# Parts of the output projection as jobs of the attention stage, edges fetched first, and two narrow one-hots in five made by GpSimd

## The chip, the cores and the metric

The kernel runs on one core of a Trainium2 chip. The metric is the device time of one execution in microseconds (us). Engines are named as in the profile: PE (TensorE), DVE (VectorE), ACT (ScalarE), POOL (GpSimd), SP (SyncE, which here only issues DMAs).

## The reference

Two layers run over 1250 nodes with 512 features; each layer adds a graph part and an attention part to x.

```python
edge_index = jnp.stack([src, dst])          # 41250 edges, sorted by dst
deg = jnp.maximum(segment_sum(ones, dst, 1250), 1.0)
x = x + L0_gnn(_layernorm(x), wc, wn, bias, edge_index)   # x@wc + mean over edges of (x@wn) + bias
x = x + L0_ffn(_layernorm(x))               # causal attention, 8 heads, then 8 gated experts
x = x + L1_gnn(_layernorm(x), src, dst, deg, W_self, W_neigh, bias, gamma, beta)
x = x + L1_ffn(_layernorm(x))               # below
# L1_ffn: x += conv3(x); q, k, v = x @ qkv_w.T + qkv_b, 8 heads of 64
logits = (q * c**-0.5) @ k.T;  _, idx = top_k(logits, 16)
attn = softmax(logits at idx);  out = attn @ v at idx
return out @ wo_w.T + wo_b
```

## The kernel before

The nodes are ten tiles of 128 rows (NT), the features four blocks of 128 (KD). Stages follow each other as blocks; in a block each engine has its own instruction stream in the order of the code, and semaphores order the engines.

**The edge stage** is `graph_in`. It builds the dense count of edges between all node pairs. SP first issues eight DMAs for src and dst (the tile `raw`), then at once those of `wc`, the biases, `wn` and the q, k, v weights; ACT issues the DMAs of X. DVE splits each edge's source into a remainder and a quotient by 128 and takes the target relative to a window (`part`, `key`); the smallest and largest give a flag that says whether every edge lies in its window. PE transposes three key blocks of three tiles each, DVE copies the result to `ends`. DVE and PE then read the flag as a register and branch: here the `Else` branch runs. It goes over 323 tiles of 128 edges (ET). For each, DVE makes two one-hots by comparing a ruler with a per-partition number: a narrow one, `hot_b`, 128 columns, and a wide one, `hot_m`, 240 columns (L263 and L264). PE multiplies them into a bank of counts (L380). Eight buffers of each are in turn (HOTS = 8), so the one-hots of tile t wait until PE has used tile t - 8 (`s_used`). Finished banks of 51 targets are copied by ACT (L466). Beside this ACT normalises the rows of X, POOL makes the rest `lo` of their split into two f16 parts (L211), and PE multiplies them with `wc`.

**The top attention stage** is `top_layer`. It goes over n = 0 to 79, that is 8 heads by 10 tiles of rows. DVE finds the 16 largest of 1250 logits of each row with two maxima and two replacements (L1683 to L1691), ACT takes exponentials, POOL subtracts, PE transposes and weighs. ACT copies the finished heads' outputs from the bank `ps_o` (`drain`), POOL scales them (`normalise`) into QO. In odd n, PE does a job in the same bank: the projections of the next heads' q, k and v, and from n = 61 the transposes of the output weight (`work_at`, `job`, ACT's `keep_job`). In the last iterations and behind them PE multiplies QO with the weight, four matmuls for each of the ten tiles (`project`), DVE adds each to X, and SP stores it.

## Time and profile before

| | us |
|---|---|
| median of 3 runs | 1689.25 (1688.99 to 1690.77) |
| the profiled execution's own time | 1686.05 |
| its span in the profile | 1684.2 |
| mean granted clock of PE | 0.966 of full speed |

The span is from the first to the last instruction of the profiled execution; its own time has some microseconds around it. Times in the rows are counted from the start of the span. A row of the order of time gives start, length, engine, line, operation, tiles and shape, and in brackets how long the engine was idle before it and what ended that.

### The profile page before, as it was taken

To read this page: it belongs to the slowest core of one execution; us is meant where nothing else is said; L and a number is where in the kernel's file an instruction comes from. 1 tells how busy PE (TensorE), PEld (TensorE's weight loads), DVE (VectorE), ACT (ScalarE), POOL (GpSimd) and SP (SyncE) were. 2 spreads that over 40 slices of the span, in tenths; PEclk is the share of its full clock that TensorE was granted. 3 is DMA by queue.
4 is the path that set the end of the run, shared out by engine and by line. 5 is a ranking of instruction groups with operands and counts; after the bars stand their busy time and mean duration, and the time that the engine had idled before them with its cause. 6 is when DMAs were issued, how large, how long until landed. Compare 5 with 4: busy or idle time off the path is not lost. (4 is left out here: it accounts for less than half of the span.)

```text
span 1684.2 us, 22128 instructions
## 1 busy us (share of the span) xinstructions
PE 1486.9 (88%) x8227; PEld 928.2 (55%) x8227; DVE 1027.9 (61%) x2001; ACT 723.4 (43%) x1396; POOL 541.6 (32%) x399
## 2 busy tenths in 40 slices
PE   4888988997878789999999899777999999998778
PEld 2444534445666654454546545455776776776554
DVE  6999233327777721113223324748999999999981
ACT  4442013225565621111111220235778778778771
POOL 0113200015565410000000060007876667577550
PEclk9999989999999999999999999889999999999999
DMA  6001000025212050000000200011101100120001
GB/s 232 1 1 79 0 1 1 0 63 158 57 39 56 9 204 24 0 0 0 1 0 0 76 1 0 1 31 33 32 1 32 32 13 20 33 53 5 1 1 61
DMA packets 28570, 57.01 MB, mean 34 GB/s; under 512 B 7904, under 2 KB 12644, under 8 KB 28208
## 3 DMA queue, kind: packets, MB, share of 16 engines
q1 hardware_dynamic: 27152, 53.03, 11.5%
q10 hardware_dynamic: 1312, 2.56, 0.4%
q8 instruction: 68, 1.11, 0.3%
q14 instruction: 38, 0.31, 0.1%
HBM read 28.77 MB, written 5.84 MB: 21 GB/s over the span
## 5 line engine op out<-in xcount | busy, mean ns | idle before, releaser
L1285 POOL TENSOR_TENSOR tl_ex<-tl_ex,tl_left 128x1250 f32<-128x1250 f32 x80 | 209.8, 2622 | 37.0 <-ACT tl_left L1587 32.9
L1126 DVE SCALAR_TENSOR_TENSOR X<-ex_ps_x,g,X 128x512 f32<-128x512 f32 x80 | 59.9, 750 | 192.6 <-PE ex_ps_x L1019 192.6
L1406 PE MATMUL tl_banks<-identf,tl_ex 128*128 128x128 f32 x800 | 139.4, 290 | 42.1 <-ACT tl_pt L1608 25.6
L1608 ACT COPY tl_pt<-tl_banks 128x512 f32<-128x512 f32 (+1 forms) x200 | 108.1, 541 | 83.8 <-PE tl_banks L1406 80.8
L992 PE MATMUL ex_ps_h<-yt,w 128*128 128x512 f32 (+1 forms) x384 | 143.8, 529 | 0.0
L1406 PEld LDWEIGHTS tl_banks<-identf,tl_ex 128*128 128x128 f32 x800 | 90.0, 144 | 97.3 <-ACT tl_pt L1608 44.3
L1019 PE MATMUL ex_ps_x<-w,hid 128*128 128x512 f32 (+1 forms) x320 | 143.1, 599 | 0.0
L1072 ACT ACTIVATE hid<-ex_ps_h,b 128x512 f32<-128x512 f32 (+1 forms) x48 | 29.1, 608 | 242.2 <-PE ex_ps_h L992 242.2
L1899 POOL TENSOR_TENSOR lo<-xn,hi 128x512 f16<-128x512 f32 x5 | 5.9, 1186 | 379.5 <-ACT hi L1989 379.5
L1587 ACT ACTIVATE tl_left<-tl_left,tl_negm 128x1250 f32<-128x1250 f32 x80 | 107.5, 1343 | 29.2 <-DVE tl_left L1691 28.8
L1683 DVE MAX8 tl_m<-tl_banks 128x8 f32<-128x1250 f32 x80 | 116.3, 1454 | 5.7 <-PE tl_banks L1383 5.6
L1689 DVE MAX8 tl_m<-tl_left 128x8 f32<-128x1250 f32 x80 | 117.1, 1464 | 2.8
L1687 DVE MATCH_REPLACE8 tl_left<-tl_m,tl_banks 128x1250 f32<-128x1250 f32 x80 | 116.0, 1450 | 0.0
L1691 DVE MATCH_REPLACE8 tl_left<-tl_m,tl_left 128x1250 f32<-128x1250 f32 x80 | 115.6, 1445 | 0.0
L992 PEld LDWEIGHTS ex_ps_h<-yt,w 128*128 128x128 f32 x384 | 74.5, 195 | 65.8 <-issue 65.6
L1581 ACT ACTIVATE tl_ex<-tl_banks,tl_negm 128x1250 f32<-128x1250 f32 x80 | 104.7, 1309 | 2.4 <-DVE tl_left L1687 1.3
L1421 PE MATMUL tl_banks<-tl_pt,tl_V 128*64 128x128 f32 x1600 | 104.8, 278 | 0.0
L1019 PEld LDWEIGHTS ex_ps_x<-w,hid 128*128 128x128 f32 (+1 forms) x320 | 60.3, 189 | 74.0 <-issue 73.9
L1421 PEld LDWEIGHTS tl_banks<-tl_pt,tl_V 128*64 128x64 f32 x1600 | 85.7, 137 | 14.2 <-issue 14.2
L264 DVE TENSOR_SCALAR hot_m<-ruler,ends 128x240 f16<-128x240 f16 x323 | 92.6, 287 | 0.2 <-issue 0.2
L1340 PE MATMUL tl_banks<-tl_ct,tl_wt 128*128 128x512 f32 (+1 forms) x192 | 82.0, 554 | 9.3 <-DVE tl_ct L1658 6.2
L624 PE MATMUL ca_banks<-wqkv,ht 128*128 128x512 f32 x160 | 76.6, 625 | 12.7 <-DVE ht L804 12.7
(272 smaller groups left out, 2935.5 us busy)
## 6 DMA issues: line engine op xcount, KB each, us to landing
...
```

The lines of the kernel that those rows point to most:

```text
L992: mm = pe.matmul(h_bank(u)[:, 0:w], w1[e][:, k, j * P:(j + 1) * P], yt[:, G % 2, k, 0:w], start=(k == 0), stop=(k == KD - 1))
L1019: mm = pe.matmul(x_bank(v)[0:rows(t), :], hid[:, (EX * G + e) % HIDS, j, r * P:r * P + rows(t)], w2[:, 2 * e + j, :], start=(j == 0), stop ...
L1285: pool.tensor_tensor(ex[:, n % EXS, 0:N], ex[:, n % EXS, 0:N], left[:, n % LEFT, :], ALU.subtract).then_inc(s_probs, 1)
L1406: mm = pe.transpose(ps_t[:, b * P:(b + 1) * P], ex[:, n % EXS, a + b * P:a + (b + 1) * P], m.identf[:, :])
L1421: mm = pe.matmul(ps_o[u * DH:(u + 1) * DH, 0:P], V[:, h // 2 % 2, k, h % 2 * DH:(h % 2 + 1) * DH], pt[:, (2 * j + u) % PTS, k * P:(k + 1) ...
L1581: act.activation(ex[:, n % EXS, 0:N], logits(n)[:, 0:N], ACT.Exp, bias=negm[:, n:n + 1]).then_inc(s_exp, 1)
L1587: act.activation(lf, lf, ACT.Exp, bias=negm[:, n:n + 1]).then_inc(s_rest, 1)
L1608: act.copy(pt[:, n % PTS, a:a + w], ps_t[:, 0:w]).then_inc(s_kept, 1)
L1683: dve.max(m8[:, n % TOPS, 0:8], logits(n)[:, 0:N]).then_inc(s_max, 1)
L1687: dve.match_replace(lf, m8[:, n % TOPS, 0:8], logits(n)[:, 0:N], TAKEN).then_inc(s_read, 1)
L1689: dve.max(m8[:, n % TOPS, 8:16], lf).then_inc(s_max2, 1)
L1691: dve.match_replace(lf, m8[:, n % TOPS, 8:16], lf, TAKEN).then_inc(s_topped, 1)
```

## The change

Top attention: four jobs that transpose the output weight move from n = 61, 63, 65, 67 to n = 57 to 63. The weight is fetched at the start of the stage, into four vectors that earlier stages have done with. New jobs "out" at n = 65, 67, ..., 79 do, for tiles 0 to 7, the three of four matmuls whose heads are done by then; ACT copies the result to `partial`, POOL adds it to X one or two iterations later. `project` has one matmul left for these tiles and four for tiles 8 and 9.

Edge stage: SP's and ACT's other DMAs wait until the edges have landed. The keys come ahead of the flag; the third key block is made in the other branch alone. POOL makes `hot_b` of tile t, from t = 8 on, where t is 1 or 3 modulo 5 and no multiple of 8: 110 of the 323 tiles. POOL waits for `s_used` of tile t - 8, and PE waits for POOL's and DVE's semaphores. POOL's other work of the stage, `shift` and the ten `lo`, stands between these one-hots.

```diff
@@ -125,6 +126,7 @@
             if t in at and (kind, at[t][0] if kind == "own" else at[t]) not in side:
                 side[kind, at[t][0] if kind == "own" else at[t]] = len(side)
 
+    by_pool = [t for t in range(HOTS, ET) if t % HOTS and t % 5 in (1, 3)]
     used, counted = [], 1
     for t in range(ET):
         counted += closes[spans(t)[-1][0]] != t
@@ -173,6 +175,7 @@
                     "(a p) -> a p", a=1)).then_inc(s_edges, 16)
+            sp.wait_ge(s_edges, 16 * 2 * (EG + 1))
             sp.dma_start(wc[:, :, :], rows_of(io["L0_gnn_wc"])).then_inc(s_wc, 16)
@@ -204,11 +207,30 @@
                                base=0, pattern=[[-1, P]], channel_multiplier=1).then_inc(s_made, 1)
             pool.affine_select(out=m.padded[:, NT - 1:NT], in_=m.padded[:, NT - 1:NT], compare_op=ALU.is_ge,
                                fill=1.0, base=TAIL - 1, pattern=[[0, 1]], channel_multiplier=-1).then_inc(s_made, 1)
-            pool.wait_ge(s_inv, 1)
-            pool.tensor_tensor(m.shift[:, :], st[:, 1, :], m.scale[:, :], ALU.mult).then_inc(s_scaled, 1)
-            for t in range(NT):
+
+            def half_hot(t):
+                pool.wait_ge(s_used, used[t - HOTS])
+                if by_pool.index(t):
+                    pool.wait_ge(s_half_hot, by_pool.index(t))
+                pool.tensor_scalar(hot_b[:, t % HOTS, :], m.ruler[:, 0:P], ends[:, 0, t:t + 1], None, ALU.is_equal
+                                   ).then_inc(s_half_hot, 1)
+
+            def shifts():
+                pool.wait_ge(s_inv, 1)
+                pool.tensor_tensor(m.shift[:, :], st[:, 1, :], m.scale[:, :], ALU.mult).then_inc(s_scaled, 1)
+
+            def low(t):
                 pool.wait_ge(s_high, t + 1)
                 pool.tensor_tensor(lo[:, t, :], xn[:, t % XR, :], hi[:, t, :], ALU.subtract).then_inc(s_low, 1)
+
+            pool.wait_ge(s_cols, 1)
+            for t in range(ET):
+                if t in by_pool:
+                    half_hot(t)
+                if t == INVERT_AT + HOTS:
+                    shifts()
+                if t - LOW_AFTER in rows_at:
+                    low(rows_at[t - LOW_AFTER])
 
         @block.vector
         def _(dve):
@@ -236,17 +258,15 @@
             dve.wait_ge(s_split, 3)
+            dve.tensor_copy(key[:, 0, :, :], part[:, 0, :, :]).then_inc(s_split, 1)
+            dve.scalar_tensor_tensor(out=key[:, 1, :, :], in0=key[:, 3, :, :], scalar=float(NT), in1=part[:, 1, :, :],
+                                     op0=ALU.mult, op1=ALU.add).then_inc(s_split, 1)
             drel = key[:, 3, :, :].rearrange("p g e -> p (g e)")
             dve.tensor_reduce(worst[:, 0:1], drel, AX_X, ALU.max).then_inc(s_flag, 1)
             dve.tensor_reduce(worst[:, 1:2], drel, AX_X, ALU.min, negate=True).then_inc(s_flag, 1)
             dve.wait_ge(s_flag, 2)
             dve.scalar_tensor_tensor(out=worst[:, 2:3], in0=worst[:, 0:1], scalar=float(1 - WIN), in1=worst[:, 1:2],
                                      op0=ALU.add, op1=ALU.max).then_inc(s_flag, 1)
-            dve.tensor_copy(key[:, 0, :, :], part[:, 0, :, :]).then_inc(s_split, 1)
-            dve.scalar_tensor_tensor(out=key[:, 1, :, :], in0=key[:, 3, :, :], scalar=float(NT), in1=part[:, 1, :, :],
-                                     op0=ALU.mult, op1=ALU.add).then_inc(s_split, 1)
-            dve.scalar_tensor_tensor(out=key[:, 2, :, :], in0=raw[:, 1, :, :], scalar=float(NT), in1=part[:, 1, :, :],
-                                     op0=ALU.mult, op1=ALU.add).then_inc(s_split, 1)
             dve.wait_ge(s_lined, 1)
             dve.tensor_reduce(flag[:, 0:1], ps_w[:, 0:P], AX_X, ALU.max).then_inc(s_flag, 1)
             dve.wait_ge(s_flag, 4)
@@ -254,13 +274,14 @@
-            dve.tensor_copy(ends[:, :, :].rearrange("p n e -> p (n e)"), ps_f[:, 0:3 * EG * P]).then_inc(s_cols, 1)
+            dve.tensor_copy(ends[:, 0:2, :].rearrange("p n e -> p (n e)"), ps_f[:, 0:2 * EG * P]).then_inc(s_cols, 1)
-                dve.tensor_scalar(hot_b[:, u, :], m.ruler[:, 0:P], b_of, None, ALU.is_equal)
+                if b_of is not None:
+                    dve.tensor_scalar(hot_b[:, u, :], m.ruler[:, 0:P], b_of, None, ALU.is_equal)
@@ -270,6 +291,11 @@
+                dve.scalar_tensor_tensor(out=key[:, 2, :, :], in0=raw[:, 1, :, :], scalar=float(NT),
+                                         in1=part[:, 1, :, :], op0=ALU.mult, op1=ALU.add).then_inc(s_split, 1)
+                dve.wait_ge(s_keyed, 2)
+                dve.tensor_copy(ends[:, 2, :], ps_f[:, 2 * EG * P:3 * EG * P]).then_inc(s_cols, 1)
+                dve.wait_ge(s_cols, 2)
@@ -287,7 +313,7 @@
-                    one_hot(t % HOTS, ends[:, 0, t:t + 1], ends[:, 1, t:t + 1], WIN * NT)
+                    one_hot(t % HOTS, None if t in by_pool else ends[:, 0, t:t + 1], ends[:, 1, t:t + 1], WIN * NT)
@@ -330,14 +356,14 @@
                     own_rows(*own_at[t])
 
             pe.wait_ge(s_made, 3)
-            pe.wait_ge(s_flag, 3)
-            pe.transpose(ps_w[:, 0:P], worst[:, 2:3], m.identf[:, :]).then_inc(s_lined, 1)
-            pe.wait_ge(s_split, 6)
-            for n in range(3):
+            pe.wait_ge(s_split, 5)
+            for n in range(2):
                 for g in range(EG):
                     c = (n * EG + g) * P
                     mm = pe.transpose(ps_f[:, c:c + P], key[:, n, g, :], m.identf[:, :])
             mm.then_inc(s_keyed, 1)
+            pe.wait_ge(s_flag, 3)
+            pe.transpose(ps_w[:, 0:P], worst[:, 2:3], m.identf[:, :]).then_inc(s_lined, 1)
             pe.wait_ge(s_cols, 1)
             pe.wait_ge(s_blank, 3)
             pe.wait_ge(s_made, 7)
@@ -376,6 +408,8 @@
                     pe.wait_ge(s_onehot, t + 1)
+                    if t in by_pool:
+                        pe.wait_ge(s_half_hot, by_pool.index(t) + 1)
@@ -393,6 +427,7 @@
             act.wait_ge(s_zeroed, 1)
+            act.wait_ge(s_edges, 16 * 2 * (EG + 1))
             for a in (0, 3, 6):
@@ -1158,8 +1193,11 @@
             work_at[2 * NT * (i - 1) + 1 + 2 * v] = ("qk", i, job)
         for v, ts in enumerate(v_groups):
             work_at[2 * NT * (i - 1) + 11 + 2 * v] = ("v", i, ts)
+    EARLY = 8
     for b in range(KD):
-        work_at[61 + 2 * b] = ("wo", b, None)
+        work_at[57 + 2 * b] = ("wo", b, None)
+    for t in range(EARLY):
+        work_at[65 + 2 * t] = ("out", t, None)
     evictions, jobs = len(v_groups), len(v_groups)
     for n in range(TN + 4):
         kept_after[n - 1], jobs_before[n] = evictions, jobs
@@ -1186,7 +1224,8 @@
-        raw_wo = space("tl_raw_wo", 40960, [P, KD, D])
+        raw_wo = (m.bias0, m.bias1, m.gamma1, m.beta1)
+        partial = space("tl_partial", 40960, [P, EARLY, D])
@@ -1236,12 +1275,12 @@
-                    if (i, half) == (3, 0):
-                        sp.wait_ge(s_job, qkv_jobs)
-                        sp.dma_start(raw_wo[:, :, :], rows_of(io["L1_ffn_wo_w"])).then_inc(s_wo_in, 16)
+                    if (i, half) == (0, 1):
+                        for b in range(KD):
+                            sp.dma_start(raw_wo[b][:, :], io["L1_ffn_wo_w"][b * P:(b + 1) * P, :]).then_inc(s_wo_in, 16)
-            sp.wait_ge(s_wo_in, 16)
+            sp.wait_ge(s_wo_in, 16 * KD)
@@ -1310,6 +1349,11 @@
+                if n - 2 in work_at and work_at[n - 2][0] == "out":
+                    t = work_at[n - 2][1]
+                    pool.wait_ge(s_job_kept, kept_after[n - 2])
+                    pool.tensor_tensor(m.X[:, t, :], m.X[:, t, :], partial[:, t, :], ALU.add).then_inc(s_added, 1)
+                    pool.wait_ge(s_added, t + 1)
@@ -1433,7 +1477,9 @@
                     pe.wait_ge(s_job_kept, kept_after[n - 1])
                     if kind == "wo":
-                        pe.wait_ge(s_wo_in, 16)
+                        pe.wait_ge(s_wo_in, 16 * KD)
+                    if kind == "out":
+                        pe.wait_ge(s_normed, (2 * HP - 3) * NT // 2 + i // 2 + 1)
                 if kind == "qk":
                     if len(what) == 1:
                         mm = project_qk(ps_o, i, what[0][0], what[0][1], part)
@@ -1445,10 +1491,15 @@
+                elif kind == "wo":
+                    mm = pe.transpose(ps_o[:, part * P:(part + 1) * P], raw_wo[i][:, part * P:(part + 1) * P],
+                                      m.identf[:, :])
-                    mm = pe.transpose(ps_o[:, part * P:(part + 1) * P], raw_wo[:, i, part * P:(part + 1) * P],
-                                      m.identf[:, :])
-                last = len(what) - 1 if kind == "v" else KD - 1
+                    if part >= HP - 1:
+                        return
+                    mm = pe.matmul(ps_o, QO[:, part, i * P:(i + 1) * P], wo[:, part, :], start=(part == 0),
+                                   stop=(part == HP - 2))
+                last = len(what) - 1 if kind == "v" else HP - 2 if kind == "out" else KD - 1
@@ -1459,8 +1510,9 @@
                     pe.wait_ge(s_final, t - 5)
-                for k in range(KD):
-                    mm = pe.matmul(proj_bank(t), QO[:, k, t * P:(t + 1) * P], wo[:, k, :], start=(k == 0),
+                ks = range(HP - 1, KD) if t < EARLY else range(KD)
+                for k in ks:
+                    mm = pe.matmul(proj_bank(t), QO[:, k, t * P:(t + 1) * P], wo[:, k, :], start=(k == ks[0]),
                                    stop=(k == KD - 1))
                 mm.then_inc(s_projected, 1)
 
@@ -1549,7 +1601,10 @@
+                elif kind == "out":
+                    act.copy(partial[:, i, :], ps_o).then_inc(s_job_kept, 1)
+                    act.wait_ge(s_job, qkv_jobs)
@@ -1703,6 +1758,8 @@
                 x_t = m.X[:, t, :]
                 dve.wait_ge(s_biased, t + 1)
+                if t < EARLY:
+                    dve.wait_ge(s_added, t + 1)
                 dve.wait_ge(s_projected, t + 1)
                 dve.tensor_tensor(x_t, x_t, proj_bank(t), ALU.add).then_inc(s_final, 1)
 
```

Three places in the order of instructions. First DVE at the start of the edge stage, from the split of the edges to the copy into `ends`, before and then after:

```order
L236 TENSOR_TENSOR key<-raw,base 128x384
L240 TENSOR_REDUCE worst<-key 128x1
L241 TENSOR_REDUCE worst<-key 128x1
L243 SCALAR_TENSOR_TENSOR worst<-worst 128x1
L245 CAST key<-part 128x384
L246 SCALAR_TENSOR_TENSOR key<-key,part 128x384
L248 SCALAR_TENSOR_TENSOR key<-raw,part 128x384
L251 TENSOR_REDUCE flag<-gi_ps_s 1x1
L253 TENSOR_SCALAR flag<-flag 1x1
L255 CAST flag_i<-flag 1x1
L257 COPY ends<-gi_ps_f 128x1152
```

```order
L258 TENSOR_TENSOR key<-raw,base 128x384
L261 CAST key<-part 128x384
L262 SCALAR_TENSOR_TENSOR key<-key,part 128x384
L265 TENSOR_REDUCE worst<-key 128x1
L266 TENSOR_REDUCE worst<-key 128x1
L268 SCALAR_TENSOR_TENSOR worst<-worst 128x1
L271 TENSOR_REDUCE flag<-gi_ps_s 1x1
L273 TENSOR_SCALAR flag<-flag 1x1
L275 CAST flag_i<-flag 1x1
L277 COPY ends<-gi_ps_f 128x768
```

The casts and keys come ahead of the reductions, one key is gone, and the copy has 768 columns. Next POOL in the edge stage, before and then after (`hot_b` x16 stands for sixteen narrow one-hots in a row):

```order
L201 MEMSET ones 128x128
L203 AFFINE_SELECT causal<-causal 128x128
L205 AFFINE_SELECT padded<-padded 128x1
L208 TENSOR_TENSOR shift<-st,scale 128x10
L211 TENSOR_TENSOR lo_57<-xn,hi_56 128x512 x10
```

```order
L206 AFFINE_SELECT causal<-causal 128x128
L208 AFFINE_SELECT padded<-padded 128x1
L215 TENSOR_SCALAR hot_b<-ruler,ends 128x128 x16
L220 TENSOR_TENSOR shift<-st,scale 128x10
L215 TENSOR_SCALAR hot_b<-ruler,ends 128x128 x5
L224 TENSOR_TENSOR lo_57<-xn,hi_56 128x512
L215 TENSOR_SCALAR hot_b<-ruler,ends 128x128 x9
L224 TENSOR_TENSOR lo_57<-xn,hi_56 128x512
```

Between two `lo` stand eight to ten narrow one-hots, and sixteen stand ahead of `shift`. Last PE at the end of top attention, from n = 79 on: L1406 and L1450 are transposes of probabilities, L1421 and L1465 the weighing, L1463 and L1515 `project`, L1500 the new job, before and then after:

```order
L1392 MATMUL tl_banks<-identf,tl_inv 64x128 x2
L1463 MATMUL tl_banks<-tl_wo,tl_QO 128x512 x8
L1406 MATMUL tl_banks<-identf,tl_ex 128x128 x8
L1421 MATMUL tl_banks<-tl_pt,tl_V 64x128 x10
L1406 MATMUL tl_banks<-identf,tl_ex 128x128 x2
L1421 MATMUL tl_banks<-tl_pt,tl_V 64x128 x10
L1463 MATMUL tl_banks<-tl_wo,tl_QO 128x512 x8
L1406 MATMUL tl_banks<-identf,tl_ex 128x128 x10
L1392 MATMUL tl_banks<-identf,tl_inv 64x128 x2
L1463 MATMUL tl_banks<-tl_wo,tl_QO 128x512 x8
L1421 MATMUL tl_banks<-tl_pt,tl_V 64x128 x20
L1463 MATMUL tl_banks<-tl_wo,tl_QO 128x512 x16
```

```order
L1500 MATMUL tl_banks<-tl_wo,tl_QO 128x512
L1515 MATMUL tl_banks<-tl_wo,tl_QO 128x512 x2
L1450 MATMUL tl_banks<-identf,tl_ex 128x128 x8
L1465 MATMUL tl_banks<-tl_pt,tl_V 64x128 x10
L1450 MATMUL tl_banks<-identf,tl_ex 128x128 x2
L1465 MATMUL tl_banks<-tl_pt,tl_V 64x128 x10
L1515 MATMUL tl_banks<-tl_wo,tl_QO 128x512 x2
L1450 MATMUL tl_banks<-identf,tl_ex 128x128 x10
L1436 MATMUL tl_banks<-identf,tl_inv 64x128 x2
L1515 MATMUL tl_banks<-tl_wo,tl_QO 128x512 x2
L1465 MATMUL tl_banks<-tl_pt,tl_V 64x128 x20
L1515 MATMUL tl_banks<-tl_wo,tl_QO 128x512 x10
```

The matmuls of `project` go from 40 to 16, of which ten are the last row.

## Rows read from the trace of the kernel before

**Rows 1.** The page, busy time of each engine.

```profile
PE 1486.9 (88%) x8227; PEld 928.2 (55%) x8227; DVE 1027.9 (61%) x2001; ACT 723.4 (43%) x1396; POOL 541.6 (32%) x399
```

**Rows 2.** Stretches: length, PE, PEld, DVE, ACT, POOL, clock, DMA.

```profile
80.00:100.00 20.00, 17.66 (x126) 10.11 (x124) 20.00 (x103) 9.70 (x16) 2.31 (x2) 1.00 0.01 1
```

**Rows 3.** Order of time, edge stage, around one `lo`.

```profile
97.47 0.24 DVE L263 TENSOR_SCALAR hot_b<-ruler,ends 128x128 f16<-128x128 f16 x1
97.63 0.27 DVE L264 TENSOR_SCALAR hot_m<-ruler,ends 128x240 f16<-128x240 f16 x1
97.82 1.21 DVE L263 TENSOR_SCALAR hot_b<-ruler,ends 128x128 f16<-128x128 f16 x1
97.83 1.16 POOL L211 TENSOR_TENSOR lo<-xn,hi 128x512 f16<-128x512 f32 x1 [8.67 <-ACT hi L429]
98.95 0.27 DVE L264 TENSOR_SCALAR hot_m<-ruler,ends 128x240 f16<-128x240 f16 x1
```

**Rows 4.** Groups on POOL by form: busy us, mean ns, idle before.

```profile
L596 POOL TENSOR_SCALAR ex_small<-ex_small,inv 128x640 f32<-128x640 f32 x8 | 15.1, 1883 | 20.6 <-DVE inv L855 20.6
...
L1314 POOL TENSOR_TENSOR X<-X,wo_b 128x512 f32<-128x512 f32 x10 | 12.8, 1277 | 0.8
...
L211 POOL TENSOR_TENSOR lo<-xn,hi 128x512 f16<-128x512 f32 x10 | 11.7, 1170 | 85.3 <-ACT hi L429 85.3
...
L579 POOL CAST kh<-kl 128x1280 fp32r<-128x1280 f32 x7 | 8.8, 1251 | 0.5
...
L596 POOL TENSOR_SCALAR ex_small<-ex_small,inv 128x128 f32<-128x128 f32 x8 | 4.8, 605 | 42.1 <-DVE inv L855 42.1
```

**Rows 5.** Order of time, edge stage, its start and DVE's end.

```profile
4.98 0.32 SPq L174 DMA_DIRECT2D raw<-in_dst  x1
...
11.40 0.36 DVE L233 TENSOR_SCALAR part<-raw 128x384 int32<-128x384 int32 x1 [7.71 <-DMA raw<-in_dst]
...
15.00 2.18 PE L339 MATMUL gi_ps_f<-identf,key 128*128 128x128 f32 x9 [0.74 <-DVE key L248]
...
17.22 1.36 DVE L257 COPY ends<-gi_ps_f 128x1152 f32<-128x1152 f32 x1 [1.74 <-PE gi_ps_f L339]
...
26.12 0.60 PE L377 MATMUL gi_ps_c<-ruler,none 128*128 128x510 f16 x1 [7.33 <-issue]
...
26.96 0.25 DVE L263 TENSOR_SCALAR hot_b<-ruler,ends 128x128 f16<-128x128 f16 x1 [4.01 <-PE gi_ps_c L380]
...
149.60 0.27 DVE L264 TENSOR_SCALAR hot_m<-ruler,ends 128x240 f16<-128x240 f16 x1
```

**Rows 6.** Order of time, end of top attention.

```profile
1632.51 0.54 ACT L1617 COPY tl_ot<-tl_banks 64x128 f32<-64x128 f32 x2
...
1666.69 14.00 PE L1463 MATMUL tl_banks<-tl_wo,tl_QO 128*128 128x512 f32 x32
...
1677.37 0.69 DVE L1707 TENSOR_TENSOR X<-X,tl_banks 128x512 f32<-128x512 f32 x1 [2.75 <-PE tl_banks L1463]
...
1680.80 0.69 DVE L1707 TENSOR_TENSOR X<-X,tl_banks 128x512 f32<-128x512 f32 x1 [2.75 <-PE tl_banks L1463]
```

**Rows 7.** Order of time, DVE: the 41st, 51st, 61st and 71st first maximum.

```profile
1393.18 1.46 DVE L1683 MAX8 tl_m<-tl_banks 128x8 f32<-128x1250 f32 x1
...
1453.41 1.46 DVE L1683 MAX8 tl_m<-tl_banks 128x8 f32<-128x1250 f32 x1
...
1516.16 1.46 DVE L1683 MAX8 tl_m<-tl_banks 128x8 f32<-128x1250 f32 x1
...
1576.39 1.46 DVE L1683 MAX8 tl_m<-tl_banks 128x8 f32<-128x1250 f32 x1
```

**Rows 8.** Order of time, causal attention: one POOL and two DVE tensor_scalar.

```profile
382.92 0.87 DVE L860 TENSOR_SCALAR ex_big<-ex_big,inv 128x1250 f32<-128x1250 f32 x1
...
402.41 1.56 POOL L596 TENSOR_SCALAR ex_small<-ex_small,inv 128x512 f32<-128x512 f32 x1 [1.38 <-DVE inv L855]
...
403.43 0.96 DVE L860 TENSOR_SCALAR ex_big<-ex_big,inv 128x768 f32<-128x768 f32 x1
```

More of the change, by code:

```diff
@@ L42 @@
 INVERT_AT = 46
+LOW_AFTER = 12
 AWAY = 1 << 20
@@ L135, in graph_in @@
         (s_made, s_zeroed, s_blank, s_edges, s_nodes, s_small, s_wc, s_base, s_split, s_flag, s_keyed, s_cols,
-         s_lined, s_flagged, s_onehot, s_used, s_closed, s_drained, s_flipped, s_kept, s_shift, s_mean, s_var, s_inv,
+         s_lined, s_flagged, s_onehot, s_half_hot, s_used, s_closed, s_drained, s_flipped, s_kept, s_shift, s_mean, s_var, s_inv,
          s_scaled, s_rows, s_high, s_low, s_side, s_side_kept) = s.signals(
-            "made zeroed blank edges nodes small wc base split flag keyed cols lined flagged onehot used closed "
+            "made zeroed blank edges nodes small wc base split flag keyed cols lined flagged onehot half_hot used closed "
             "drained flipped kept shift mean var inv scaled rows high low side side_kept")
@@ L348, in _ @@
             with pe.If(scattered):
+                pe.wait_ge(s_split, 6)
+                for g in range(EG):
+                    c = (2 * EG + g) * P
+                    mm = pe.transpose(ps_f[:, c:c + P], key[:, 2, g, :], m.identf[:, :])
+                mm.then_inc(s_keyed, 1)
+                pe.wait_ge(s_cols, 2)
                 for c in range(NC):
@@ L1170, in top_layer @@
     v_kept = [len(v_groups)] + [kept_after[2 * NT * (i - 1) + 11 + 2 * (len(v_groups) - 1)] for i in range(1, HP)]
-    qkv_jobs = jobs_before[61]
+    qkv_jobs = jobs_before[57]
     with ExitStack() as ctx:
@@ L1175, in top_layer @@
         (s_zn, s_w_turned, s_w_kept, s_x_turned, s_x_kept, s_edge, s_tapped, s_mid, s_conv, s_first, s_first_kept,
-         s_job, s_job_kept, s_wo_in, s_staged_k,
+         s_job, s_job_kept, s_wo_in, s_added, s_staged_k,
          s_fetched_0, s_fetched_1, s_staged, s_scored, s_max, s_negm, s_read, s_max2, s_topped, s_exp, s_rest,
@@ L1179, in top_layer @@
          s_projected, s_final, s_stored) = s.signals(
-            "zn w_turned w_kept x_turned x_kept edge tapped mid conv first first_kept job job_kept wo_in staged_k "
+            "zn w_turned w_kept x_turned x_kept edge tapped mid conv first first_kept job job_kept wo_in added staged_k "
             "fetched_0 fetched_1 staged scored max negm read max2 topped exp rest sum inv blank probs turned kept "
```

## Prediction

> **What bounds the kernel now.** I read the page first, then a table of stretches, then the order of time in three places. The page puts PE at 88% and DVE at 61% of the span [rows 1]; that is an average over stages, so the stages are read one by one. The change touches the first stage (the adjacency from the edges) and the last one (top attention).
>
> In the edge stage DVE is the bound: from 80 to 100 us it is busy 20.00 of 20 us, PE 17.66, POOL 2.31 [rows 2]. In the order of time DVE starts a narrow one-hot, 0.16 us later a wide one, 0.19 us later the next narrow one: 0.355 us a tile [rows 3]. The same rows show something else. POOL starts one `lo` subtraction at 97.83, and the DVE instruction started at 97.82 takes 1.21 us instead of 0.24: the next starts at 98.95. So a POOL operation of 1.16 us stopped DVE for 0.97 us. Each of the ten `lo` operations (mean 1.170 us, [rows 4]) has one such stretched DVE instruction beside it, and there are no others. The sum closes: from 26.96 to 149.60 us [rows 5] are 122.6 us; 315 tiles at 0.355 are 111.8 and ten stops of 0.97 are 9.7; 1.1 us is one wait for PE. DVE waits for almost nothing else there.
>
> Ahead of it the stage has a start-up chain [rows 5]: the last edge DMA is issued at 4.98, DVE begins on the edges at 11.40, PE transposes nine key blocks from 15.00, DVE copies 1152 columns at 17.22, PE then comes to its branch, and its first product follows at 26.12 after 7.33 us in which it waited for nothing that the profile shows. DVE goes on at 26.96 once PE has used tile 0.
>
> At the end PE is the bound: 32 records of the output projection, which are 16 matmuls, take 14.00 us back to back, and DVE's last two additions, one behind each four matmuls, start at 1677.37 and 1680.80 [rows 6]: 3.43 us for four, 0.86 us a matmul. In between, in the top stage, DVE sets the pace.
>
> **The change part by part.**
>
> *Output projection.* For tiles 0 to 7 three of four matmuls leave the tail: 24 x 0.86 = 20.6 us of PE. Some comes back. The job of n = 79 stands in the last iterations: its third matmul, 0.86 us, is still in line ahead of the projections, and its first must wait until ACT has drained the bank (ACT's two copies from 1632.51, [rows 6]), which holds up the transposes behind it by about 1.0 us. Tail: -18.7 us, bounds -20.6 (nothing comes back) and -15 (three or four more such waits of 1.0 in n = 80 to 82, where ACT has a copy more).
> In the odd n from 65 to 79 PE gets 2.6 us, ACT a copy, POOL an addition of 1.28 us [rows 4]. I cost these at nothing. The cover is DVE's pace: from the 41st to the 51st maximum, where PE does q and k jobs with four matmuls each and POOL stages the next head, DVE needs 1453.41 - 1393.18 = 60.23 us; from the 61st to the 71st, with only small jobs, 1576.39 - 1516.16 = 60.23 us [rows 7]. A job of three matmuls is smaller than one of four. POOL's addition has its twin in the first ten iterations, where `wo_b` is added at 1.28 us each. Were this cover gone, a slip of 0.5 us in eight iterations would cost 4 us.
> The weight's DMA goes to the start of the stage and its transposes go four iterations earlier, where ACT and PE have the same room: nothing.
>
> *Start.* Edges go first, alone. The last, of 136 bytes, is issued from 4.98 to 5.30. From DVE's last addition at 1680.80 (0.69 us long) to the end of the span a transfer has 2.7 us; so the edges are in at about 7.7 instead of 11.40, with bounds 7.0 and 9.5: -3.7 us. The chain behind loses a third of the transposes (0.7 of 2.18) and of the copy (0.4 of 1.36) and a key on DVE, but the flag now comes last: I take -1.5. These 5.2 us reach PE's branch. The 7.33 us behind it are no part of the change. If they are spent on reading the program, they now fall while X and the weights, both held back, fill the queues; I let 0.7 us be lost to that. Start: -4.5 us, bounds 0 (the whole gain is eaten before 26.12) and -6.5. X lands later too, near 19 to 20 instead of 14.8. ACT then has its 20 reductions done by about 36 to 37 and DVE needs them at tile 46, near 38: covered, by little; without it 1 to 2 us.
>
> *One-hots on POOL.* 110 of 323 narrow one-hots leave DVE: 110 x 0.165 = -18.2 us. They don't come free. POOL's `lo` stops DVE for its length less 0.20 us. That the same holds for a tensor_scalar with a per-partition scalar, the form that moves, is in [rows 8]: beside one on POOL from 402.41 to 403.97, DVE's from 403.43 with 768 columns ends at 404.39. At the rate of its 1250 columns in 0.87 us it needs about 0.62, so it really began at 403.77, which is POOL's end less 0.20.
> How long is the new operation? No row has is_equal on f16 on POOL. The nearest has the same form and size, 128x128 with a per-partition scalar: 0.605 us; 640 columns take 1.883 [rows 4]. This gives a stop of 0.605 - 0.20 = 0.40 us, more than the 0.165 saved: 110 x (0.40 - 0.165) = +25.9 us. Bounds: below, a cast's 1.251/1280 = 0.98 ns per column in place of (1.883 - 0.605)/512 = 2.50 gives 0.605 - 128 x 1.52 = 0.41 us, a stop of 0.21 and +5 us; still lower, 0.13 (the fixed part cheaper too) and -4 us. Above, a stop of the whole 0.605: +48 us. I take 0.40, since form and size agree.
> By the Trainium skill (SBUF — State Buffer, on which operations grab the shared pair) a tensor_scalar in a 2-port mode and a GpSimd instruction exclude each other for a whole instruction. The trace agrees, with 0.97 of 1.16 us, and this speaks against the change: a model with no exclusion would have -18 in place of +26.
> PE gets a second wait a tile, but POOL may run eight tiles ahead (8 x 0.4 us), and its three or four operations in that time need about 2.4 us: hidden. The one wait for PE (1.1 us) goes in part: -0.5.
>
> *Sum.* -18.7 - 4.5 + 25.9 - 0.5 = +2.2 us, on a profiled execution of 1686.05 us (span 1684.2). That one is 3.2 us below the median of the timed runs, 1689.25; I put the same difference on the median: **1691.5 us**. The two halves nearly cancel, and each 0.1 us in the stop is 11 us of time. About 0.2% (3.4 us) is what a measurement of this kernel can tell from no change.
>
> **The rivals.**
> *A, POOL as its nearest row* (stop 0.34 to 0.46): 1685 to 1698. For it: form and size. Chance 0.50.
> *B, POOL is cheap.* The operation takes 0.33 to 0.54 us, a stop of 0.13 to 0.34. Then it adds -4 to +19 us and the total is -28 to -4.5, 1662 to 1685. For it: casts and copies on POOL have 0.98 ns per column. Against it: a tensor_scalar has 2.50 between 128 and 640 columns [rows 4]. By the Trainium skill (GPSIMD Engine Reference, Engine selection) one-input work on GpSimd is roughly line-rate; that is this rival, and the tensor_scalar rows here differ from it by a factor of 2.5. Chance 0.25.
> *C, the stop is longer* (the compare dearer than a product, or DVE held for the whole operation): from a stop of 0.41 us on the kernel is slower by over 0.2%, and at 0.605 it ends at 1689.25 + 48 - 23.7 = 1714. Chance 0.17 for a stop above 0.46.
> *D, the top stage slips*: PE's 2.6 us and POOL's addition make DVE wait in the odd n. Against it the equal 60.23 us; for it that POOL has a normalisation and an addition one behind the other. At 0.5 to 1 us in eight iterations +4 to +8, about 1697. Chance 0.08.
> *That the projections' gain fails to come* would need PE idle in the tail for other reasons; the 32 records without a gap speak against it.
>
> **How the numbers follow.** A lies on both sides: of its 0.50 I put 0.27 within 0.2%, 0.20 slower, 0.03 faster. B is faster, C and D slower. Faster 0.28, same 0.27, slower 0.45. The time is A's. The range leaves out the cheap half of B and the upper part of C: 1674 to 1707; A's own is 1685 to 1698.
>
> **What would show it.** The edge stage: DVE's wide one-hots of about 0.6 us beside POOL's new ones, some 110 of them, and a mean time on POOL near 0.6 us; the distance from DVE's tile 8 to its last wide one-hot near 148 us instead of 122.6. PE's first product near 21.6. The top stage: 60.2 us for ten maxima up to the end. The tail: from the 71st maximum to the last addition 85.7 us, where it is 1680.80 - 1576.39 = 104.4 now. I am wrong if POOL's operation is shorter than 0.5 us, if DVE is not stopped by it, or if PE's first product stays at 26.

## The result and the profile after

The changed kernel takes 1666.42 us (median of 4 runs, 1663.35 to 1669.27), the kernel before 1689.25 in the same comparison: ratio 0.9864, 95% interval 0.9846 to 0.9883. It is about 23 us (1.4%) faster, where 1691.5, 2 us slower, was forecast. A fourth run of before at 2983.76 us is an outlier and isn't used; with it the median would be 1690.01. The profiled execution took 1665.02 us, span 1663.2, clock 0.968.

The page of after, busy time of each engine, to be set beside [rows 1]: PE and DVE fell by 14 and 11 us, POOL rose by 93.

```profile
PE 1473.0 (89%) x8224; PEld 923.3 (56%) x8224; DVE 1017.1 (61%) x1890; ACT 726.9 (44%) x1404; POOL 634.2 (38%) x517
```

*The start.* The order of time of after, for the events of [rows 5] (last long edge DMA, the edges on DVE, transposes, copy, first product, DVE at tile 8, DVE's last wide one-hot):

```profile
4.22 0.38 SPq L174 DMA_DIRECT2D raw<-in_dst  x1
4.64 0.26 SPq L176 DMA_DIRECT2D raw<-in_dst  x1
6.05 0.36 DVE L255 TENSOR_SCALAR part<-raw 128x384 int32<-128x384 int32 x1 [2.35 <-DMA raw<-in_dst]
...
8.15 1.51 PE L363 MATMUL gi_ps_f<-identf,key 128*128 128x128 f32 x6 [8.15 <-DVE key L262]
...
10.47 0.94 DVE L277 COPY ends<-gi_ps_f 128x768 f32<-128x768 f32 x1
...
18.86 0.61 PE L409 MATMUL gi_ps_c<-ruler,none 128*128 128x510 f16 x1 [7.24 <-issue]
...
19.71 0.26 DVE L284 TENSOR_SCALAR hot_b<-ruler,ends 128x128 f16<-128x128 f16 x1 [3.86 <-PE gi_ps_c L414]
...
144.15 0.27 DVE L285 TENSOR_SCALAR hot_m<-ruler,ends 128x240 f16<-128x240 f16 x1
```

DVE stands at tile 8 at 19.71 instead of 26.96: -7.25 us. Of this 5.35 is the edges' landing (11.40 to 6.05), 1.82 the chain from there to the end of the copy (7.18 to 5.36), and 0.08 the rest.

*The edge tiles.* From tile 8 to the last wide one-hot 122.64 us became 124.44. The forecast was 148. Here is a stretch of the order of time, DVE and POOL rows only. A row with x2 is two wide one-hots one behind the other, because the narrow one of the second tile is made by POOL.

```profile
27.75 0.24 DVE L284 TENSOR_SCALAR hot_b<-ruler,ends 128x128 f16<-128x128 f16 x1
27.91 0.27 DVE L285 TENSOR_SCALAR hot_m<-ruler,ends 128x240 f16<-128x240 f16 x1
27.96 0.77 POOL L215 TENSOR_SCALAR hot_b<-ruler,ends 128x128 f16<-128x128 f16 x1 [0.17 <-POOL hot_b L215]
28.10 0.24 DVE L284 TENSOR_SCALAR hot_b<-ruler,ends 128x128 f16<-128x128 f16 x1
28.26 0.54 DVE L285 TENSOR_SCALAR hot_m<-ruler,ends 128x240 f16<-128x240 f16 x2
28.68 0.24 DVE L284 TENSOR_SCALAR hot_b<-ruler,ends 128x128 f16<-128x128 f16 x1
...
97.31 1.36 DVE L285 TENSOR_SCALAR hot_m<-ruler,ends 128x240 f16<-128x240 f16 x2
97.36 1.23 POOL L224 TENSOR_TENSOR lo<-xn,hi 128x512 f16<-128x512 f32 x1
...
98.59 0.24 DVE L284 TENSOR_SCALAR hot_b<-ruler,ends 128x128 f16<-128x128 f16 x1
```

Beside POOL's one-hot of 0.77 us, DVE's starts are 0.16, 0.19, 0.16 and 0.42 apart: the last is two wide ones at 0.19 and 0.04 us more. A `lo` still stops DVE: 98.59 - 97.31 = 1.28 us for the two, 0.90 too long. From 42 to 143 us I took each distance between DVE's starts, less 0.165 or 0.19 an instruction; what is left, apart from gaps of 0.5 us and more, is about 7 us, so 0.07 to 0.08 us for each of the 92 POOL one-hots in it.

So in place of the forecast's 44 us of stops (110 x 0.40) stand about 8. The largest new item is a wait that I had priced at "1 to 2 us":

```profile
24.70 0.63 ACT L439 ACTIVATE hi<-X 128x512 f16<-128x512 f32 x1 [14.29 <-DMA X<-in_x]
...
39.33 1.28 ACT L453 ACT_TABLE_LOAD   x1
40.62 0.30 ACT L453 ACTIVATE st<-st,eps 128x10 f32<-128x10 f32 x1
...
40.96 0.22 DVE L290 RECIPROCAL scale<-st 128x10 f32<-128x10 f32 x1 [7.83 <-ACT st L453]
```

X came at 24.70, ACT finished its twenty reductions and a table load at 40.62, and DVE, at tile 46 since 33, stood 7.83 us. The groups on POOL, by form (busy, mean, idle before), show the new operation at 747 ns. Of the 31.0 us put down to PE, 17.3 lie ahead of the first one-hot; how full POOL is in the stretch stands under *Three in five*.

```profile
L215 POOL TENSOR_SCALAR hot_b<-ruler,ends 128x128 f16<-128x128 f16 x110 | 82.2, 747 | 41.7 <-PE gi_ps_c L414 31.0 <-POOL hot_b L215 10.6
L224 POOL TENSOR_TENSOR lo<-xn,hi 128x512 f16<-128x512 f32 x10 | 12.1, 1214 | 0.0
```

*Top attention and the tail.* From the 61st to the 71st first maximum are 60.25 us, where [rows 7] had 60.23, and from the 71st to the 80th 54.26, where before had 54.24: the new jobs of n = 65 to 79 cost DVE nothing. The order of time at the end (the 71st and 80th maximum, the last projections, the last addition), to be set beside [rows 6]:

```profile
1573.99 1.46 DVE L1738 MAX8 tl_m<-tl_banks 128x8 f32<-128x1250 f32 x1
...
1628.25 1.45 DVE L1738 MAX8 tl_m<-tl_banks 128x8 f32<-128x1250 f32 x1
...
1650.93 8.85 PE L1515 MATMUL tl_banks<-tl_wo,tl_QO 128*128 128x512 f32 x20
...
1656.46 0.69 DVE L1764 TENSOR_TENSOR X<-X,tl_banks 128x512 f32<-128x512 f32 x1 [2.72 <-PE tl_banks L1515]
1659.89 0.69 DVE L1764 TENSOR_TENSOR X<-X,tl_banks 128x512 f32<-128x512 f32 x1 [2.75 <-PE tl_banks L1515]
```

From the 71st maximum to the last addition are 85.90 us (104.41 before): -18.5. The whole: -7.25 + 1.8 - 18.5 = -23.95. The profiled spans differ by 21.0; the other 2.9 is a longer way between the edge stage and top attention (997.2 to 1000.1 us), where the change does nothing. In the traces of the experiments, with the same code there, it is between 997.2 and 1005.4 us, so 2.9 says nothing of the change.

### The profile page after: what moved, and what is told of

Its sections match the earlier page's. It is cut to its first block and busy times, and to the rows that moved or that the text cites. A ratio compares the mean times of both kernels' runs of the same rounds, so it can differ in the third digit from the quotient of the medians.

```text
span 1663.2 us, 22381 instructions
## 1 busy us (share of the span) xinstructions
PE 1473.0 (89%) x8224; PEld 923.3 (56%) x8224; DVE 1017.1 (61%) x1890; ACT 726.9 (44%) x1404; POOL 634.2 (38%) x517
## 5 line engine op out<-in xcount | busy, mean ns | idle before, releaser
L1450 PE MATMUL tl_banks<-identf,tl_ex 128*128 128x128 f32 x800 | 136.5, 285 | 22.4 <-ACT tl_pt L1663 11.2
L1450 PEld LDWEIGHTS tl_banks<-identf,tl_ex 128*128 128x128 f32 x800 | 89.0, 142 | 85.6 <-issue 44.7
L1465 PE MATMUL tl_banks<-tl_pt,tl_V 128*64 128x128 f32 x1600 | 104.8, 278 | 0.0
L215 POOL TENSOR_SCALAR hot_b<-ruler,ends 128x128 f16<-128x128 f16 x110 | 82.2, 747 | 41.7 <-PE gi_ps_c L414 31.0
L1465 PEld LDWEIGHTS tl_banks<-tl_pt,tl_V 128*64 128x64 f32 x1600 | 85.7, 137 | 14.1 <-issue 14.1
```

Source lines behind the costliest of these rows:

```text
L1450: mm = pe.transpose(ps_t[:, b * P:(b + 1) * P], ex[:, n % EXS, a + b * P:a + (b + 1) * P], m.identf[:, :])
L1465: mm = pe.matmul(ps_o[u * DH:(u + 1) * DH, 0:P], V[:, h // 2 % 2, k, h % 2 * DH:(h % 2 + 1) * DH], pt[:, (2 * j + u) % PTS, k * P:(k + 1) ...
```

## The experiments

Each ratio is to the kernel before on the same chip, in the same comparison. The medians come from several chips, with 1689.25 for before beside the change, 1688.01 beside 3 in 10 and three in five, 1691.45 beside the last two, and 1687.84 beside the others; so the ratios are what can be compared. "Stretch" is DVE's time from tile 8 to its last wide one-hot in the profiled execution.

| kernel | median, ratio to before (95%) | tile 8 | stretch | DVE's wait for the variance |
|---|---|---|---|---|
| before | 1687.84 | 26.96 | 122.6 | 0 |
| the change | 1666.42, 0.9864 (0.9846-0.9883) | 19.71 | 124.4 | 7.8 |
| none on POOL | 1669.41, 0.9887 (0.987-0.9905) | 20.55 | 129.6 | 7.8 |
| edge stage only | 1685.21, 0.9989 (0.9975-1.0002) | 20.09 | 123.5 | 7.8 |
| x at once | 1663.88, 0.9846 (0.9827-0.9866) | 24.86 | 116.3 | 1.3 |
| x, then weights | 1657.88, 0.9819 (0.98-0.9839) | 18.41 | 116.9 | 1.7 |
| the same, 3 in 10 | 1657.48, 0.9808 (0.9782-0.9834) | 18.34 | 116.7 | 1.3 |
| three in five | 1693.1, 1.0016 (0.9999-1.0033) | 19.47 | 148.4 | 7.1 |
| 3 in 10, `lo` on DVE | 1659.52, 0.982 (0.9791-0.9849) | 19.8 | 113.6 | 0.5 |
| 2 in 5, `lo` on DVE | 1657.92, 0.9806 (0.9778-0.9833) | 19.6 | 113.4 | 0.4 |

(For the last two tile 8 is worked out from tile 0 plus 8 x 0.355, since DVE had no gap there. The two kernels with probes, below, ran once each and are read by their traces alone.)

**The price of a POOL one-hot: none on POOL.**

```diff
-    by_pool = [t for t in range(HOTS, ET) if t % HOTS and t % 5 in (1, 3)]
+    by_pool = []
```

> The changed kernel with an empty list of tiles for GpSimd: VectorE builds all 278 narrow one-hots again. The rest of the change stays. Theory of the prediction (a narrow one-hot on GpSimd stops VectorE for 0.40 us and saves it 0.165): taking the 110 off gives 110 x 0.235 = 26 us back, about 1640 us, and VectorE's stretch from tile 8 to the last wide one-hot falls from 124.4 to about 98 us. Theory now (the trace of the changed kernel shows VectorE standing only some 0.03 us longer at each, while GpSimd starts one every 0.93 us without a gap, so GpSimd and the wait for ScalarE's variance make up the stretch): VectorE then bounds the stretch at about its pace of before, 122.6 us of before with the ScalarE stall of 8 us in it added or partly hidden: 122 to 131 us, total 1663 to 1673.

Measured, from tile 8, the variance and the last wide one-hot:

```profile
20.55 0.25 DVE L284 TENSOR_SCALAR hot_b<-ruler,ends 128x128 f16<-128x128 f16 x1 [4.57 <-PE gi_ps_c L414]
...
42.05 0.22 DVE L290 RECIPROCAL scale<-st 128x10 f32<-128x10 f32 x1 [7.83 <-ACT st L453]
...
150.17 0.27 DVE L285 TENSOR_SCALAR hot_m<-ruler,ends 128x240 f16<-128x240 f16 x1
```

The stretch is 129.6 us, as the second theory has it (all 323 narrow one-hots are DVE's here; the 278 above is a slip). With 110 of them on POOL it is 5.2 us shorter, not 26 longer. Both kernels have the variance wait, and without it they are 121.8 and 116.6. The prediction's stop of 0.40 is refuted. But 5.2 is less than 110 x (0.165 - 0.07) = 10.5: behind tile 8 DVE's waits for PE are 0.4 us here and 6.2 in the changed kernel, and that closes the account (10.5 - 5.8 = 4.7). At the two longest of these waits in the changed kernel, 1.5 us each, PE had itself waited 1.6 us for ACT's copy of a bank; so what takes half of the gain back is in part the rest of the chain, not POOL. In the totals the difference is about 3 us of 1666; the intervals of the two ratios overlap, and it is not resolved.

**Is it POOL's rate? Three in five.**

```diff
+    by_pool = [t for t in range(HOTS, ET) if t % HOTS and t % 5 in (1, 3, 4)]
```

> The changed kernel, but GpSimd makes the narrow one-hot of three tiles in five (t % 5 in 1, 3, 4) in place of two in five, some 165 tiles. Theory now, GpSimd is the bound at 0.925 us each: 55 more of them make the stretch 45 to 51 us longer, total about 1711 to 1717. Theory of the prediction, 0.40 us of VectorE's time for each and 0.165 saved: 55 x 0.235 = 13 us longer, about 1679. Rival that both are cheap: 55 x 0.165 = 9 us shorter, about 1657.

Measured: +26.7 us by the medians, +24.0 in the stretch, between the expectations. The groups of this kernel's POOL:

```profile
L215 POOL TENSOR_SCALAR hot_b<-ruler,ends 128x128 f16<-128x128 f16 x165 | 109.2, 662 | 46.6 <-PE gi_ps_c L414 25.7 <-POOL hot_b L215 20.9
L224 POOL TENSOR_TENSOR lo<-xn,hi 128x512 f16<-128x512 f32 x10 | 11.6, 1162 | 0.0
```

How full POOL is can't be read from what its idle time is put down to. The order of time of the changed kernel, POOL rows:

```profile
99.39 0.77 POOL L215 TENSOR_SCALAR hot_b<-ruler,ends 128x128 f16<-128x128 f16 x1 [0.17 <-POOL hot_b L215]
100.33 0.80 POOL L215 TENSOR_SCALAR hot_b<-ruler,ends 128x128 f16<-128x128 f16 x1 [0.17 <-PE gi_ps_c L414]
...
104.06 0.77 POOL L215 TENSOR_SCALAR hot_b<-ruler,ends 128x128 f16<-128x128 f16 x1 [0.17 <-PE gi_ps_c L414]
105.74 0.69 POOL L215 TENSOR_SCALAR hot_b<-ruler,ends 128x128 f16<-128x128 f16 x1 [0.91 <-PE gi_ps_c L414]
```

Between two of these one-hots there are at least 0.17 us, whoever is named for them; only what is longer is time in which POOL had nothing to do. Gaps over 0.2 us add up to 5.2 us in the stretch of 148.4 at three in five, 3.8 of them around the variance wait: POOL is the bound. At two in five they are 15.5 of 124.4 us, 8.7 of them around that wait. So in the changed kernel too POOL runs back to back for all but 6.8 of the 116.6 us: it is nearly full, and so is DVE. My "theory now" was right in that, and wrong in the price of one more. I had taken 0.925 us each from a stretch of ten microseconds; with less of DVE's work beside it the operation takes 0.66 instead of 0.75, and the idle time was there to be used.

**Three in ten**, on the kernel of *X, then weights* below.

```diff
+    by_pool = [t for t in range(HOTS, ET) if t % HOTS and t % 10 in (1, 4, 7)]
```

> The kernel with the order edges, x, weights, and GpSimd makes the narrow one-hot of about three tiles in ten (t % 10 in 1, 4, 7; never t % 8 = 0) in place of two in five. Theory now: GpSimd at one every 0.925 us bounds the stretch of edge tiles where it makes two in five (2.5 tiles in 0.925 us, 0.37 us a tile); at three in ten VectorE bounds it, and is 3 to 7 us faster than the same kernel with two in five. Rival, if VectorE bounds the stretch at two in five already: slower by the share that is taken back, 28 x 0.165 = 5 us.

Measured: 116.7 against 116.9 us, 1657.48 against 1657.88: no difference. DVE gets 24 one-hots back (4.0 us less the stops) and its waits for PE fall from 4.8 to 1.0 us. Neither expectation held: what DVE has more to do, it waits less. The two kernels ran on different chips; their ratios (0.9808 and 0.9819) agree within their intervals.

**Where the edges, X and the weights stand: x at once.**

```diff
             act.wait_ge(s_zeroed, 1)
-            act.wait_ge(s_edges, 16 * 2 * (EG + 1))
```

> The changed kernel without ScalarE's wait for the edges: the rows of x are asked for at once, as in the kernel before; the weights on SyncE's queue still stand behind the edges. If the late landing of x (ScalarE's first mean at 24.7 us) is what makes VectorE stand 8 us at tile 46 for the variance: that wait is gone, but x runs beside the edges on the DMA engines, so VectorE starts on the edges later than 6.05 us, by 2 to 5 us. Total 1660 to 1664. Rival: the stall at tile 46 is covered by GpSimd's chain of narrow one-hots, which then bounds the stretch alone, and the total is that of the changed kernel plus the lost start, 1668 to 1671.

Measured, edges, X and variance:

```profile
10.86 0.36 DVE L255 TENSOR_SCALAR part<-raw 128x384 int32<-128x384 int32 x1 [7.17 <-DMA raw<-in_dst]
12.85 0.63 ACT L438 ACTIVATE hi<-X 128x512 f16<-128x512 f32 x1 [6.61 <-DMA X<-in_x]
...
38.00 0.22 DVE L290 RECIPROCAL scale<-st 128x10 f32<-128x10 f32 x1 [1.26 <-ACT st L452]
```

X is there at 12.85, the wait for the variance falls from 7.8 to 1.3 us and the stretch by 8.1. The edges land at 10.86 and DVE starts tile 8 at 24.86: of the start's 7.25 us only 2.1 are left. So POOL's chain doesn't stand behind the wait, and the rival falls.

**X, then weights.**

```diff
             sp.wait_ge(s_edges, 16 * 2 * (EG + 1))
+            sp.wait_ge(s_nodes, 64)
             sp.dma_start(wc[:, :, :], rows_of(io["L0_gnn_wc"])).then_inc(s_wc, 16)
```

> The changed kernel, and SyncE also waits for the four transfers of x before it asks for the weights, so the order is edges, x, weights. The start on the edges stays at about 6.05 us. If x is late because the weights share the DMA engines with it: x lands at 14 to 17 us, ScalarE's first mean comes then, the 8 us that VectorE stands for the variance at tile 46 fall to 0 to 2, total 1657 to 1660. Rival: GpSimd's own chain bounds the stretch (110 one-hots every 0.925 us and nine lo of 1.2 us are 113 us, and they went on during the stall as far as the buffers allow), so the total falls by 4 us or less, or the weights now come late for the first products of the edge stage's rows, 1664 to 1668.

Measured: 8.5 us below the change by the medians, 7.6 by the ratios, and 8.8 by the trace of the edge stage (7.5 in the stretch, 1.3 ahead of it), as the first theory has it. The spans are 7.1 apart: in this execution the tail took 1.6 us more at a granted clock of 0.94 instead of 1.00, as it did in the profiled ones of *x at once* and *3 in 10* (0.95). The order of time of this kernel:

```profile
15.73 0.63 ACT L440 ACTIVATE hi<-X 128x512 f16<-128x512 f32 x1 [5.47 <-DMA X<-in_x]
...
17.56 0.61 PE L410 MATMUL gi_ps_c<-ruler,none 128*128 128x510 f16 x1 [5.92 <-issue]
...
31.99 0.22 DVE L291 RECIPROCAL scale<-st 128x10 f32<-128x10 f32 x1 [1.72 <-ACT st L454]
```

X comes 9 us earlier with the weights out of its way, DVE waits 1.7 us instead of 7.8, and PE's unexplained idle ahead of its first product is 5.92 instead of 7.24 us. That the weights are what held X up rests on this run, which moves nothing but SP's transfers of weights and biases.

**The tail alone against the edges alone.** The function `top_layer` is that of before.

```diff
-    EARLY = 8                      # and all of the change in top_layer
```

> The changed edge stage with the last layer (output projection, its weights, its tail) of the kernel before. If the tail's 18.5 us is the early output projection and adds up with the rest: from the 80th maximum to the last addition 50.2 us as before, total 1666.4 + 18.5 = 1685 us, 0.997 of before. If the two parts are not additive (for instance because jobs in the last layer slow its stages): 1680 or less, or 1690.

Measured 1685.21. Its median is 18.8 us above that of the change, though on another chip; by the ratios, 0.9989 and 0.9864, the tail is worth 21 us give or take 4. Its trace has 50.17 us from the 80th maximum to the last addition, as before (50.17), and the change's has 31.64: 18.5. The edge stage's whole change comes to 0.1% by the runs (0 to 4 us), not told from nothing, while the trace has DVE's last wide one-hot 6.0 us earlier. Within that the parts add up.

**What stops DVE: two probes.** The seven forms stand in the places t % 5 == 2; shown is one.

```diff
+    pool.wait_ge(s_used, used[t - HOTS])
+    op = pool.tensor_scalar(junk16[:, 0:P], m.ruler[:, 0:P], col, None, ALU.is_equal)
```

> The changed kernel with no narrow one-hot on GpSimd, and 42 extra instructions on GpSimd whose results nobody reads, one every five edge tiles from tile 72 to 277, six of each of seven forms in this order: tensor_scalar of f16 128 wide, tensor_scalar of f32 128 wide, tensor_tensor of f16 128 wide, tensor_tensor of f32 128 wide, tensor_scalar of f16 384 wide, tensor_scalar of f32 384 wide, copy of f32 384 wide. It measures how long each stops VectorE's train of one-hots. Theory now: an instruction with one tensor input does not stop VectorE (under 0.1 us each, whatever the width), one with two tensor inputs stops it for most of its own time (lo, 512 wide, stopped it 0.95 of 1.2 us; 128 wide then 0.2 to 0.5 us). Rival: what decides is the type or the width, and the f32 forms or the 384 wide forms of tensor_scalar stop it too, by most of their time.

> A second probe as the first: no narrow one-hot on GpSimd, and 42 extra f32 instructions there whose results nobody reads, one every five edge tiles from tile 72 to 277, six of each: tensor_scalar 64, 192 and 256 wide, tensor_tensor 256 and 384 wide, copy 128 and 256 wide. Theory from the first probe (tensor_scalar stopped VectorE for 0.07 us at 128 columns and 0.47 to 0.49 at 384; tensor_tensor for 0.25 to 0.28 at 128 and 1.0 at 512; copy for 0.32 at 384): the stop is proportional to the columns moved and depends on the form: 0.06, 0.2 and 0.3 us for the three tensor_scalar, 0.5 and 0.75 for tensor_tensor, 0.11 and 0.21 for copy. Rival, the prediction's rule of the length less 0.20 us for every form: tensor_scalar 0.4 to 0.9 us, copy 0.1 to 0.25, tensor_tensor 0.5 to 0.75.

The order of time of the first probe, around an operation with one tensor input and around one with two (DVE and POOL rows):

```profile
51.07 0.71 POOL L239 TENSOR_SCALAR junk<-ruler,ends 128x128 f16<-128x128 f16 x1 [1.12 <-PE gi_ps_c L443]
51.07 0.27 DVE L314 TENSOR_SCALAR hot_m<-ruler,ends 128x240 f16<-128x240 f16 x1
51.26 0.31 DVE L313 TENSOR_SCALAR hot_b<-ruler,ends 128x128 f16<-128x128 f16 x1
51.49 0.37 DVE L314 TENSOR_SCALAR hot_m<-ruler,ends 128x240 f16<-128x240 f16 x1
51.68 0.24 DVE L313 TENSOR_SCALAR hot_b<-ruler,ends 128x128 f16<-128x128 f16 x1
...
73.47 0.45 POOL L243 TENSOR_TENSOR junk<-ruler 128x128 f16<-128x128 f16 x1 [0.95 <-PE gi_ps_c L443]
73.49 0.51 DVE L314 TENSOR_SCALAR hot_m<-ruler,ends 128x240 f16<-128x240 f16 x1
73.92 0.24 DVE L313 TENSOR_SCALAR hot_b<-ruler,ends 128x128 f16<-128x128 f16 x1
```

The longer operation costs DVE 0.23 - 0.16 = 0.07 us, the shorter one 0.43 - 0.19 = 0.24. The mean delays taken so over each group of five or six (length on POOL / DVE's delay, us; f32 unless said):

| columns | tensor_scalar | tensor_tensor | copy |
|---|---|---|---|
| 64 | 0.60 / 0.02 | | |
| 128 | 0.73 / 0.07 (f16 0.71 / 0.07) | 0.50 / 0.28 (f16 0.45 / 0.25) | 0.35 / 0.08 |
| 192 | 0.88 / 0.14 | | |
| 256 | 1.10 / 0.25 | 0.76 / 0.54 | 0.43 / 0.21 |
| 384 | 1.35 / 0.49 (f16 1.33 / 0.47) | 1.02 / 0.81 | 0.55 / 0.32 |
| 512 (`lo`) | | 1.18 / 0.97 | |

Single delays differ by where DVE stands when the operation begins: 0.08 to 0.19 for the tensor_scalar of 192 columns, 0.21 to 0.30 at 256, 0.06 to 0.12 for the copy of 128. "Length less 0.20 us" holds to 0.03 for tensor_tensor at every width, is near for copies (0.22 to 0.27 less), and wrong for tensor_scalar by 0.4 to 0.7 us. The f16 and f32 forms agree. My guess of the first probe, that one tensor input costs nothing at any width, was wrong at 384 columns. The second probe's figures came out near the expected ones, and the rival's rule is out for tensor_scalar. "Proportional to the columns" holds for tensor_tensor (2.1 ns a column up to 384), not for tensor_scalar (0.3 ns at 64 columns, 1.3 at 384). On DVE's side it was always the same train of f16 one-hots; other operations there were not probed.

**`lo` on DVE.** The ten `lo` leave POOL for DVE, 18 tiles behind their rows.

```diff
-                pool.tensor_tensor(lo[:, t, :], xn[:, t % XR, :], hi[:, t, :], ALU.subtract).then_inc(s_low, 1)
+                dve.tensor_tensor(lo[:, t, :], xn[:, t % XR, :], hi[:, t, :], ALU.subtract).then_inc(s_low, 1)
```

> The kernel with three tiles in ten on GpSimd and the order edges, x, weights, and in it the ten lo (xn minus hi, 128x512) of the edge stage are made by VectorE in place of GpSimd, 18 tiles after their rows in place of 12. On GpSimd each of them stopped VectorE for 0.97 us; on VectorE the same operation took 0.68 us where the later stage has it. Theory (VectorE's train is the bound and a two-input operation on GpSimd stops it for most of its length): 10 x 0.29 = 2.9 us off the stretch of 116.7 us, total 1654 to 1655.5. Rival: the waits between TensorE, ScalarE and VectorE bound the stretch once VectorE has room, or VectorE now stands for ScalarE's hi: 1656.5 to 1659.

> The same with two tiles in five on GpSimd. It takes ten operations of 1.2 us off GpSimd too, so GpSimd's narrow one-hots come back in time: the short waits of VectorE and TensorE that made two in five no better than three in ten (some 4 us) should shrink. Theory: 3 to 6 us off the stretch of 116.9 us, total 1652 to 1655. Rival: TensorE waits for the narrow one-hots because each of them takes 0.75 us, not because of lo, and the result is that of three in ten or worse by 1 us.

Measured: the stretch is 3.1 and 3.5 us shorter, with 0.68 us for the operation on DVE against a stop of 0.97. The sizes are as expected, but not for that alone: 0.8 and 1.3 us of them are a shorter wait for the variance, since DVE came to tile 46 later. DVE's waits for PE didn't shrink either: 1.0 to 2.6 us at three in ten, 4.8 to 4.7 at two in five, where the second expectation had them go. The totals don't show the gain: 0.982 and 0.9806 of before, within the intervals of the kernels without it, and the medians, 1659.52 and 1657.92, are above the 1655.5 and 1655 forecast at most. Part was lost at the start. To place the `lo` in the branch that isn't taken, I had written its loop out, and at three in ten DVE now reached tile 0 at 16.95 instead of 13.03, after 5.47 us of waiting for nothing the profile shows; that the loop is the cause was not tried by itself. So it isn't better in a way that these runs can tell.

## Why the prediction was wrong

**The step that failed** is "*One-hots on POOL* ... This gives a stop of 0.605 - 0.20 = 0.40 us ... +25.9 us". The length was even longer than assumed (0.747 us). What failed is the rule that turned it into a stop, taken from `lo`, a tensor_tensor, to a tensor_scalar. The stop was 0.07 us, below the lowest bound of 0.13. The term was 110 x (0.07 - 0.165) = -10.5 us instead of +25.9, and waits for PE (6.2 us, 0.4 with none on POOL) took back about half of it.

A second step failed beside it: POOL's three or four operations in eight tiles were put at 2.4 us and "hidden". With 0.75 us each and the 0.17 between two, which the sum left out, three are 2.8 us, as long as DVE takes for eight tiles at 0.355, and POOL was nearly full. The waits for PE, forecast at -0.5, rose by 4.9.

[Rows 8] were the evidence that the rule holds for a tensor_scalar, and they were misread. The overlap was 0.54 us and DVE lost 0.34 of it. I read that as "held for all but the last 0.20". They say equally that DVE runs on at a reduced rate; the probes show 0.25 us lost in 1.10 at 256 columns, 0.49 in 1.35 at 384. That fits, but the DVE operation of [rows 8] (f32, 768 columns) was not probed. And 512 columns say nothing of 128: the delay per column grows from 0.5 ns at 128 columns to 1.3 at 384. The rule of the Trainium skill (SBUF — State Buffer, Who interferes with whom) that a tensor_scalar in a 2-port mode on DVE and a GpSimd instruction exclude each other for a whole instruction is near for a tensor_tensor on POOL (0.97 of 1.18 us) and disagrees for a tensor_scalar there (0.07 of 0.73); the measurement decides.

Rival B had the outcome right (1662 to 1685) for the wrong reason: not a short operation but one that doesn't hold DVE. By the Trainium skill (GPSIMD Engine Reference, Engine selection) one-input work is near line rate there; at 128 columns it took 0.75 us, where DVE starts the next after 0.16, so that reason fails.

**Start: right in kind, under-sized.** -7.25 against -4.5, outside the bound of -6.5. The edges landed at 6.05, not 7.7: the store of a whole tile of X after the last addition was a poor model of 136 bytes. The chain gave 1.82 for 1.5, and PE's idle of 7.33 stayed (7.24), so that the 0.7 us put down to full queues didn't come.

**X late: right place, wrong size.** Forecast at 19 to 20 and a wait of 1 to 2 us if uncovered; it was 24.70 and 7.8. X shared the DMA engines with the weights, which I hadn't counted: with the weights behind it, it came at 15.73. So holding the transfers back gave 7.25 us at the start and took 7.8 at tile 46: by itself it brought nothing, and the 5.45 us by which the edge stage ends earlier are about what the moved one-hots bring (5.2).

**Right:** the tail (-18.7 forecast, -18.5 measured, and 18.5 again between the traces of the change and of the edges alone), 85.7 us from the 71st maximum to the last addition (85.90), and no cost of the new jobs under DVE's pace (60.25 for 60.23).

The sum with measured terms: tail -18.5, start -7.25, one-hots saved -18.2, stops +7.7, the variance +7.8, more waiting for PE +4.9, together -23.6. The medians are 22.8 apart and the profiled spans 21.0. The last four terms add up to +2.2 for a stretch that grew by 1.8.
